# First stage of a two-layer image kernel: its 3x3 convolution from three fp32r products to plain fp32 in four column groups, and the product back in four row groups

## The reference

```python
pf = relu(einsum('bhwc,kc->bhwk', x, W1) + b1)                # 48 -> 16 channels
pf = einsum('bhwk,jk->bhwj', pf, W2) + b2
mask = softmax(einsum('bhwk,mk->mbhw', pf, mask_token) over the pixels)
mwf = (mask.sum(0)[..., None] * pf).sum(axis=(1, 2))          # 16 numbers for each image
conv_w = (einsum('bk,ok->bo', mwf, Wh) + bh).reshape(B, 16, 16, 3, 3)
xp = quick_gelu(einsum('bhwc,dc->bhwd', x, Wd) + bd)          # 48 -> 16 channels
xc = conv3x3(xp, conv_w)                                      # each image has its own weights
x1 = einsum('bhwd,cd->bhwc', quick_gelu(xc), Wu) + bu + x     # 16 -> 48 channels
```

## Time and profile before

| | us |
|---|---|
| median of 3 executions | 3405.01 |
| lowest and highest | 3398.68, 3407.35 |
| the profiled execution | 3408.9 |
| its span in the profile | 3407.0 |

### The profile page before, as it was taken

The page is one execution under the profiler, slowest core; times in us unless marked ns, Lnnn a source line. Parts: engine busy times, 40 slices in busy tenths (PEclk is TensorE's granted clock), DMA queues, the critical chain, the costliest instruction groups (busy, mean ns, idle before and its releaser), DMA issues. The chain is left out here.

```text
span 3407.0 us, 98870 instructions
## 1 busy us (share of the span) xinstructions
PE 3144.9 (92%) x35124; PEld 1981.8 (58%) x35124; DVE 2619.1 (77%) x4249; ACT 2320.6 (68%) x4196; POOL 1860.1 (55%) x2059
## 2 busy tenths in 40 slices
PE   6988879999999999999999999995999999999998
PEld 2664465555555555555555555553666666666665
DVE  4535526777777777777777777775999999999998
ACT  3413416888888888888888888873666666666665
POOL 1101115666666666666666666662555555555554
PEclk7988887999999999999999999996999999999999
DMA  4412121111111111111111111115666656566573
GB/s 123 114 44 70 57 72 30 43 43 45 46 45 43 43 43 44 47 45 43 43 43 44 47 45 45 43 37 82 120 102 106 108 100 117 98 106 115 93 119 56
DMA packets 235801, 230.41 MB, mean 68 GB/s; under 512 B 118064, under 2 KB 230704, under 8 KB 232624
## 3 DMA queue, kind: packets, MB, share of 16 engines
q1 hardware_dynamic: 235696, 229.19, 33.0%
HBM read 151.32 MB, written 77.76 MB: 67 GB/s over the span
## 5 line engine op out<-in xcount | busy, mean ns | idle before, releaser
L596 POOL TENSOR_TENSOR kex<-ks,cw 112x294 f32<-112x294 f32 x1024 | 740.9, 748 | 419.0 <-ACT ks L909 419.0
L1066 DVE TENSOR_TENSOR s<-ps_s,bias 113x588 f32<-113x588 f32 x512 | 390.4, 762 | 127.9 <-PE ps_s L683 127.8
L1311 POOL TENSOR_TENSOR ya_lo<-ya,ya_hi 128x464 fp32r<-128x464 f32 x224 | 284.3, 1269 | 314.4 <-DVE ya_hi L1481 212.8
L699 PE MATMUL ps_t<-cw,s 113*98 113x113 f32 x3072 | 406.1, 269 | 0.2 <-ACT pt L939 0.2
L1073 DVE TENSOR_REDUCE mx<-s 113x12 f32<-113x588 f32 x512 | 391.1, 764 | 13.3
L699 PEld LDWEIGHTS ps_t<-cw,s 113*98 113x98 f32 x3072 | 291.5, 129 | 184.6 <-issue 179.3
L1317 POOL TENSOR_TENSOR hid_a_lo<-hid_a,hid_a_hi 128x448 fp32r<-128x448 f32 x224 | 298.5, 1333 | 179.7 <-ACT hid_a_hi L1408 179.7
L714 PEld LDWEIGHTS ps_o<-vs,pt 98*49 98x49 f32 x12288 | 306.6, 127 | 151.3 <-issue 100.0
L683 PE MATMUL ps_s<-kex,q 48*49 48x294 f32 x4096 | 372.5, 422 | 0.0
L932 ACT ACTIVATE s<-s 113x588 f32<-113x588 f32 x512 | 338.7, 685 | 48.6 <-POOL s L590 48.5
L939 ACT ACTIVATE pt<-ps_t 98x588 f32<-98x588 f32 x512 | 332.8, 650 | 52.6 <-PE ps_t L699 52.5
(11 more groups left out here) (174 smaller groups left out, 7254.2 us busy)
## 6 DMA issues: line engine op xcount, KB each, us to landing
ya<-y_chunks SPq DMA_DIRECT2D x64, 532.9 KB, 6.1
y_chunks<-y SPq DMA_DIRECT2D x256, 76.1 KB, 1.9
xin<-x_chunks SPq DMA_DIRECT2D x256, 73.5 KB, 2.5
xres<-x_chunks SPq DMA_DIRECT2D x256, 73.5 KB, 1.9
x_chunks<-xo SPq DMA_DIRECT2D x256, 73.5 KB, 1.8
out<-xr SPq DMA_DIRECT2D x32, 588.0 KB, 5.3
yb<-y_chunks SPq DMA_DIRECT2D x96, 177.6 KB, 8.2
xr<-x_chunks SPq DMA_DIRECT2D x32, 514.5 KB, 5.6
```

What stands on the lines that cost most here:

```text
L596: ins = pool.tensor_tensor(kex[a][:, win, :, :], ks[:, win, :].unsqueeze(1).to_broadcast([PP, HEADS, N]), w("head").unsqueeze(2).to_broadc ...
L699: mm = pe.transpose(ps_t[0:2 * N, i, j * 2 * BO:j * 2 * BO + QP], s_sb[d][:, i, part], w("ident"))
L1066: dve.tensor_tensor(s_sb[d][:, :, :], ps_s[0:QP, :, 0:HN], bias[:, low, int(d == DUOS - 1), :].unsqueeze(1).to_broadcast([QP, 2, HN]), ALU ...
```

## The change

The fp32r splitting goes away from the first program, and with it `down_hi`, `down_lo`, `conv_hi`, `conv_lo`, `cw_hi`, `cw_lo`, `cwt_hi`, `cwt_lo`, `wu_hi`, `wu_lo`, ACT's copies, all of POOL's work in the loop and DVE's hi and lo weights.

- `down` is one fp32 tensor of 96 partitions: three times the 32 channels of an image pair, shifted by -1, 0 and +1 rows, for four pairs side by side in the free dimension, 56 rows of 58 pixels. ACT writes the middle 32 partitions directly. SP copies them with DMAs to the lower and upper 32 partitions, in two portions (rows 0 to 30 after four chunks, the rest after seven), two DMAs each.
- The weights come from 36 plain fp32 matmuls into 96 partitions (one column group for each vertical tap, 48 columns for each pair), and one DVE instruction spreads them to `cwt` with the new constant `same_half`.
- The convolution is three horizontal taps for each pair, 96 rows by 32 columns, and the four pairs write to four column groups of one bank.
- The product back is one plain fp32 matmul for each pair, from the pair's 32 rows of `mid`, to its own bank. All four wait together for DVE's four updates of the chunk before, and DVE waits for the last of the four.

```diff
+COPY = 4
@@ constants
+    "spread_ci": (D, 128), "same_half": (P1, 2),
@@ tiles
+        down = sb("down", [P1, PAIRS, H, W + 2])
+        cwt = sb("cwt", [P1, PAIRS, 3, 2, D])
@@ SP
+            def copy_rows(g):
+                if g > 0:
+                    sp.wait_ge(conv_done, g * C1)
+                for start, end, chunks in ((0, COPY * R1 - 1, COPY), (COPY * R1 - 1, H - 1, C1)):
+                    sp.wait_ge(down_done, (g * C1 + chunks) * 2)
+                    sp.dma_start(down[0:2 * D, :, start + 1:end + 1, :], down[2 * D:4 * D, :, start:end, :]).then_inc(down_rows_in, 16)
+                    sp.dma_start(down[4 * D:P1, :, start:end, :], down[2 * D:4 * D, :, start + 1:end + 1, :]).then_inc(down_rows_in, 16)
             for g in range(GROUPS):
                 k = g % 2
+                copy_rows(g)
                 store(k, g)
@@ POOL
+            pool.memset(down[2 * D:4 * D, :, :, 0:W + 2:W + 1], 0.0).then_inc(pad_zero, 1)
+            pool.memset(down[0:2 * D, :, 0, :], 0.0).then_inc(pad_zero, 1)
+            pool.memset(down[4 * D:P1, :, H - 1, :], 0.0).then_inc(pad_zero, 1)
@@ PE, weights
-                    for s in range(2):
-                        pe.matmul(ps[5][:, 0:TAPS * D], mrep[:, s, :, :].rearrange("q i c -> q (i c)"), wh[:, s, :],
-                                  start=s == 0, stop=False)
-                    pe.matmul(ps[5][:, 0:TAPS * D], w("spread_ci"), w("bh"), start=False, stop=True).then_inc(cw_done, 1)
+                    for p in range(PAIRS):
+                        for kh in range(3):
+                            rows, taps = slice(2 * D * kh, 2 * D * (kh + 1)), slice(3 * D * kh, 3 * D * (kh + 1))
+                            part = ps[5][rows, 3 * D * p:3 * D * (p + 1)]
+                            for s in range(2):
+                                pe.matmul(part, mrep[:, s, 2 * p:2 * p + 2, :].rearrange("q i c -> q (i c)"), wh[:, s, taps],
+                                          start=s == 0, stop=False)
+                            mm = pe.matmul(part, w("spread_ci")[:, 0:2 * D], w("bh")[:, taps], start=False, stop=True)
+                    mm.then_inc(cw_done, 1)
+                    pe.wait_ge(cwt_set, g + 1)
+                    pe.wait_ge(down_done, (g * C1 + C1) * 2)
+                    pe.wait_ge(down_rows_in, g * 64 + 64)
@@ PE, convolution
-                            for i, (weights, image) in enumerate(((cwt_hi, down_hi), (cwt_hi, down_lo), (cwt_lo, down_hi))):
-                                if c == 0 and i == 2:
-                                    pe.wait_ge(cwt_set, g + 1)
-                                for t in range(TAPS):
-                                    mm = pe.matmul(ps[c % 2][:, 0:T1], weights[:, t, :, :].rearrange("q i c -> q (i c)"),
-                                                   image[:, c * R1 + t // 3:c * R1 + t // 3 + R1, t % 3:t % 3 + W],
-                                                   start=i == 0 and t == 0, stop=i == 2 and t == TAPS - 1)
+                            for kw in range(3):
+                                for p in range(PAIRS):
+                                    mm = pe.matmul(ps[c % 2][2 * D * p:2 * D * (p + 1), 0:T1],
+                                                   cwt[:, p, kw, :, :].rearrange("q i c -> q (i c)"),
+                                                   down[:, p, c * R1:(c + 1) * R1, kw:kw + W], start=kw == 0, stop=kw == 2)
                             mm.then_inc(conv_done, 1)
@@ PE, product back
                         if c >= 1:
-                            pe.wait_ge(conv_split, g * C1 + c)
+                            pe.wait_ge(gelu_done, g * C1 + c)
+                            if c >= 2:
+                                pe.wait_ge(x1_done, (g * C1 + c - 1) * PAIRS + 1)
                             for p in range(PAIRS):
-                                if c >= 2:
-                                    pe.wait_ge(x1_done, (g * C1 + c - 2) * PAIRS + p + 2)
-                                rows = slice(p * P1, (p + 1) * P1)
-                                for i, (weights, image) in enumerate(((wu_hi, conv_hi), (wu_lo, conv_hi), (wu_hi, conv_lo))):
-                                    mm = pe.matmul(ps[2 + p][0:P1, 0:T1], weights[:, rows], image[:, (c - 1) % 2, :],
-                                                   start=i == 0, stop=i == 2)
-                                mm.then_inc(up_done, 1)
+                                rows = slice(p * 2 * D, (p + 1) * 2 * D)
+                                mm = pe.matmul(ps[2 + p][0:P1, 0:T1], w("wu")[rows, p * P1:(p + 1) * P1],
+                                               mid[rows, (c - 1) % 2, :], start=True, stop=True)
+                            mm.then_inc(up_done, 1)
@@ ACT, chunk stage
-                            if c >= 2:
-                                act.wait_ge(down_split, g * C1 + c - 1)
...
-                                    ins = act.activation(mid[rows, c % 2, :], ps[2 * (c % 2) + q][64 * i + 32:64 * i + 64, 0:T1],
-                                                         ACT.Gelu_apprx_sigmoid, bias=w("bd")[rows, :])
+                                    ins = act.activation(down[2 * D:4 * D, 2 * q + i, c * R1:(c + 1) * R1, 1:1 + W],
+                                                         ps[2 * (c % 2) + q][64 * i + 32:64 * i + 64, 0:T1].rearrange(
+                                                             "q (r n) -> q r n", r=R1),
+                                                         ACT.Gelu_apprx_sigmoid, bias=w("bd")[2 * D:4 * D, :])
@@ DVE
+                    dve.tensor_tensor(cwt[:, :, :, :, :].rearrange("q p t i c -> q (p t) i c"),
+                                      ps[5][0:P1, 0:PAIRS * 3 * D].rearrange("q (t c) -> q t c", c=D).unsqueeze(2).to_broadcast(
+                                          [P1, PAIRS * 3, 2, D]),
+                                      w("same_half").unsqueeze(1).unsqueeze(3).to_broadcast([P1, PAIRS * 3, 2, D]),
+                                      ALU.mult).then_inc(cwt_set, 1)
                     for c in range(C1):
                         for p in range(PAIRS):
-                            dve.wait_ge(up_done, (g * C1 + c) * PAIRS + p + 1)
+                            if p == 0:
+                                dve.wait_ge(up_done, g * C1 + c + 1)
```

More of the change, by code:

```diff
@@ L156, in layer0 @@
         rep_done, mrep_done, cw_done = sem("rep_done"), sem("mrep_done"), sem("cw_done")
-        cw_hi_set, cw_lo_set, cwt_hi_set, cwt_set = sem("cw_hi_set"), sem("cw_lo_set"), sem("cwt_hi_set"), sem("cwt_set")
+        cwt_set = sem("cwt_set")
         conv_done, gelu_done, up_done, x1_done = sem("conv_done"), sem("gelu_done"), sem("up_done"), sem("x1_done")
@@ L208, in _ @@
         def _(pool):
[L210 to L218, removed]
-                for c in range(C1):
-                    pool.wait_ge(conv_hi_set, g * C1 + c + 1)
-                    pool.tensor_tensor(conv_lo[:, c % 2, :], mid[:, c % 2, :], conv_hi[:, c % 2, :],
-                                       ALU.subtract).then_inc(conv_split, 1)
+            pool.memset(down[2 * D:4 * D, :, :, 0:W + 2:W + 1], 0.0).then_inc(pad_zero, 1)
+            pool.memset(down[0:2 * D, :, 0, :], 0.0).then_inc(pad_zero, 1)
+            pool.memset(down[4 * D:P1, :, H - 1, :], 0.0).then_inc(pad_zero, 1)
         @block.tensor
@@ L226, in _ @@
             pe.wait_ge(weights_in, 16)
-            pe.wait_ge(wu_set, 1)
             with pe.Fori(0, GROUPS // 2) as gg:
@@ L301, in _ @@
             act.wait_ge(weights_in, 16)
-            act.wait_ge(pad_zero, 1)
+            act.wait_ge(pad_zero, 3)
             with act.Fori(0, GROUPS // 2) as gg:
@@ L329, in _ @@
                         if c >= 2:
-                            act.wait_ge(up_done, (g * C1 + c - 1) * PAIRS)
+                            act.wait_ge(up_done, g * C1 + c - 1)
                         act.activation(mid[:, c % 2, :], ps[c % 2][:, 0:T1], ACT.Gelu_apprx_sigmoid).then_inc(gelu_done, 1)
-                        act.wait_ge(gelu_done, g * C1 + c + 1)
-                        act.activation(conv_hi[:, c % 2, :], mid[:, c % 2, :], ACT.Copy).then_inc(conv_hi_set, 1)
         @block.vector
@@ L385, in _ @@
                     dve.wait_ge(cw_done, g + 1)
-                    conv_weights = ps[5][:, 0:TAPS * D].rearrange("q (t c) -> q t c", t=TAPS)
-                    dve.tensor_copy(cw_hi[:, :, :], conv_weights).then_inc(cw_hi_set, 1)
-                    dve.wait_ge(cw_hi_set, g + 1)
-                    dve.tensor_tensor(cw_lo[:, :, :], conv_weights, cw_hi[:, :, :], ALU.subtract).then_inc(cw_lo_set, 1)
-                    image = w("image")
-                    for i in range(GI):
-                        ins = dve.tensor_scalar(cwt_hi[:, :, i, :], cw_hi[:, :, :], image[:, i:i + 1], None, op0=ALU.mult)
-                    ins.then_inc(cwt_hi_set, 1)
-                    dve.wait_ge(cw_lo_set, g + 1)
-                    for i in range(GI):
```

(8 more changed lines are left out.)

13 lines of the change are left out of this document (1 added, 12 removed).

## The result

| | before | after |
|---|---|---|
| median, us | 3405.01 | 3299.32 |
| lowest and highest | 3398.68, 3407.35 | 3299.0, 3308.36 |
| the profiled execution | 3408.9 | 3299.0 |

After over before is 0.9702, 95% interval 0.967 to 0.9734: 105.7 us less by the medians, where 90 were forecast.

What follows compares the result with a forecast made beforehand. The prediction took PE alone to bound the convolution stretch. Per group 29.2 - 6.9 + 0.6 = 22.9 us saved, times 4 less 1.6 gives 90, so 3315 us from the median; range 3280 to 3345 (chance 0.65).

Steps and rivals of the forecast that it cites:

- What bounds the stretch: Convolution stretch: PE alone before; after, DVE's updates between products set a chunk period of 3.6 us.
- Convolution: Each chunk's convolution: 5.68 us of fp32r matmuls replaced by six slots of plain fp32, 2.41 us.
- rival 2: Convolution's column groups run only two by two: 8 us saved for each group, 3373 us; chance 0.11.
- Product back: Each chunk's product back: 2.45 us replaced by four plain fp32 matmuls in row groups, 0.90 us.
- The stretch: Convolution and projection back, each group: 29.8 us against 59.0, so 29.2 saved, the clock rising some 5 us in.
- Weights: Making each group's convolution weights: 72 small rows in about 11 us, 11.9 against 5.0 in all, 6.9 lost.
- Chunk stage: Projection, features and logits: ACT's copy and POOL's subtraction removed, DVE sets the pace; 0.6 us saved for each group.
- Copies: SP's four SBUF-to-SBUF copies for each group, 3.27 MB, 13 us at 250 GB/s, hidden and costed at nothing.
- rival 1: Clock stays at 1.2 GHz through the convolution: 3.5 us saved for each group, 3391 us; chance 0.14.
- copies aren't late (4): Rival that SBUF copies end after the convolution's start: about 3470 us at 40 GB/s; chance 0.03.
- rival 3: Plain fp32 tiles run one after the other: chunk 12.5 us, 38 lost for each group, 3555 us; chance 0.04.

Runs made afterwards that it cites:

- the kernel after once more: The changed kernel run again with nothing changed: 3305.68 us median, ratio 0.9718 to the kernel before.

## Why the prediction was right, and where it was off

The forecast was 90 us less, the first program gave 99.6 (100.2 to the first load of attention), and the time lay inside the range. Going through the sum:

- **What bounds the stretch.** Right: PE alone before; afterwards the loop through DVE. Forecast for a chunk 3.6 us, measured 3.58. PE's own share, 3.31, was shown as 3.33 in every second chunk of the run in which each product waits for its own bank.
- **Convolution.** 2.41 us forecast, 2.40 measured. The four column groups run side by side as the earlier trace rows had it for two, and for two by two. Had they run two by two, rival 2's sum (3373) would have been 12 us too high by the run that does it, 3360.85. What the prediction didn't see is that it hangs on the order of issue.
- **Product back.** 0.90 forecast, 0.94 measured.
- **The stretch.** 29.8 forecast (7.3, 21.6 and 0.9), 30.15 measured: 7.42 to the first product (81.36 to 88.78), 21.51 for six periods (to 110.29), 1.22 for the last product. The clock rose after 5.6 us and not 5, and the prediction had no wait ahead of the last product. Ahead of the last product PE has nothing to do and waits 2.58 us for DVE; in it or behind it the clock falls, as the next stage begins at 1.2 GHz (its first rows take 1.01 us, where the median of that line is 0.54).

```profile
107.79 2.45 DVE L384 SCALAR_TENSOR_TENSOR xt<-pa,cw,xt 96x448 f32<-96x448 f32 x4 [1.13 <-PE pa L293]
110.29 1.29 PE L293 MATMUL pa<-mid,cw 32*96 32x448 f32 x8 [2.58 <-DVE xt L384]
111.51 1.01 PE L237 MATMUL pa<-xt,cw 96*64 96x448 f32 x2
```

- **Weights.** This is the term that was mis-sized: 6.9 us lost for each group forecast, 4.83 measured (9.83 against 5.00), 8.3 us over four groups. By the prediction's sum the 72 rows take 10.6 us, rounded up to 11; they took 9.0. A row cost 0.08 and not 0.09, and a change of shape 0.13 and not 0.17. The 0.17 comes of a misreading of the earlier trace rows: it takes the mean of 0.48 us of the earlier trace rows for the last of L270's four rows. Of the four, the first lasts 0.61 us and the others 0.44, so the last one began at 72.60, its columns were through at 72.84, and L272 began 0.13 later. The weights are most of the 10 us by which the first program beat the sum. The chunk stages gave another 4, by luck (next point), and some 2 were lost in the stretches and behind the last of them.
- **Chunk stage.** 0.6 saved for each group forecast. From the first projection to the mask's product it took 39.5, 38.6 and 37.0 us before (groups 1 to 3) and 36.1, 36.1 and 37.3 after, 5.6 less in three groups instead of 1.8 (and group 0's, with the loads in it, 47.4 and 46.9). But the kernel after once more took 36.1, 37.2 and 39.1. The stretches differ with their clock; an effect of ACT's and POOL's removed work doesn't show. Here are two of 39 us, the first of before (its group 1), the second of after once more (its group 3):

```profile
135.86:175.37 39.51, 28.91 (x85) 8.68 (x85) 28.44 (x48) 30.84 (x46) 7.42 (x7) 0.83 0.60 162
```

```profile
290.84:329.97 39.13, 30.46 (x89) 8.85 (x85) 30.20 (x50) 26.88 (x39) 0.00 (x0) 0.81 0.55 127
```

  So the 0.6 can't be told from nothing here; DVE set the pace, as the prediction said. What the first program gained beyond that here is the clock's and not the change's.
- **Copies.** Nothing forecast, nothing measured. They move their 3.27 MB at 180 to 215 GB/s, a little under the 250 that stood for them.
- **Attention.** Not in the sum and rightly so: the 10.6 us that the one profile shows go with the clock, which comes up at another time in another execution of the same kernel. The two sets of runs say the same: 105.7 us by the medians of the first, 95.7 (3401.34 less 3305.68) by those of the last, with the forecast's 90 and the first program's 100 beside them.
- **The rivals.** The clock did rise in the convolution (rival 1), column groups don't run two by two or in line (2, 3), copies aren't late (4). The row groups of the product work side by side, as its 0.94 us show: eight rows in line would take 3. In line it would have been slower than before, as rival 3 said, but at 3477 and not 3555: its chunk had the product back in line too (12.5 us), where in the run with one column group the row groups still ran side by side (9.14 for the convolution and 0.94 for the product, 10.1).

## What to carry to other kernels

Three fp32r products can be dearer than one plain fp32 product whose tiles fill the array: count slots (rows over the tiles that run side by side), not matmuls. Matmuls of different tiles are best issued next to one another, with the loop over tiles innermost (57 us here for four tiles and six rows each; with three tiles, runs of six rows overlapped nearly in full), and with no change of tile shape between them, not even for a tiny bias matmul (23 us here). Before a gain or loss of 10 us is put down to a change, look in the trace whether it lies in the code that was changed.

## What the runs showed of the hardware

- Four column groups of 32 columns, fed from the same 96 rows of partitions, do the same rows 3.8 times as fast as one (2.40 against 9.14 us), new weights for each row included.
- With six rows in line for each column group, the next group begins with the third of them, although it is issued behind the sixth: four groups take 4.72 us.
- A change of tile shape costs some 0.13 us at 1.2 GHz by itself (0.21 between the starts of two rows where 0.08 is usual), and the side-by-side work across it: 72 small rows take 9.0 us with 24 changes and 2.3 without.
- TensorE stayed at 1.2 GHz for the first 14 to 57 us of attention's code, in the same kernel 25 us in one execution and 37 in another. Over the twelve profiles attention took 1818.4 to 1838.6 us.
- Copies within SBUF of 32 partitions ran at 180 to 215 GB/s, beside busy engines.
